# The context's keys, values and output matrix computed beside the q, k, v projection instead of inside the attention turns

## What is computed

```python
x = x + attention(layernorm(x), Wqkv, ...)        # q, k, v = clip(ln(x) @ Wqkv.T); 32 heads, causal, alibi
x = x + cross(layernorm(x), ctx, ctx, Wq, Wk, Wv, Wo, bo, g)
x = x + ffn(layernorm(x), ...)                    # 4-bit weights, hidden size 2752

def cross(q, k, v, ...):                          # per tile: arrays are 128 x 1024
    qh = softmax(Wq q over the 64 of a head) * SCALE
    kh = softmax(Wk k over the 1024 columns)      # 512 x 1024
    vh = Wv v
    context = kh vh^T per head                    # 8 blocks of 64 x 64
    out = Wo (context^T qh) + bo                  # then a norm over 128, times g
```

## Time and profile before

| | |
|---|---|
| median of 3 runs | 3303.19 us (3303.15 to 3303.97) |
| span of the profiled execution, first to last instruction | 3299.9 us |
| what lies around the span, against the median | 3.3 us |
| phase 1, first product to last | 24.07 to 561 us |
| phase 2, first turn to the last | 589 to about 1802 us |
| phase 3 | from about 1816 us |
| PE busy over the span | 3128.8 us (95%) |
| DVE, ACT, POOL busy | 1773.3, 1045.8, 507.1 us |

### The profile page before, as it was taken

How to read it: one execution, slowest core, us unless ns; L and a number is a source line. 1 busy time by engine, 2 the same in 40 slices (tenths; PEclk the granted TensorE clock), 3 DMA queues, 4 the chain that set the end, 5 groups by cost and what they waited for, 6 DMA issues and landing times. The chain is left out here.

```text
span 3299.9 us, 41826 instructions
## 1 busy us (share of the span) xinstructions
PE 3128.8 (95%) x15136; PEld 2393.9 (73%) x15136; DVE 1773.3 (54%) x2927; ACT 1045.8 (32%) x2356; POOL 507.1 (15%) x525
## 2 busy tenths in 40 slices
PE   7999997799999999999996799999999899999998
PEld 6888886566666666666663688888887788888887
DVE  5311112466666666666663655555555655555555
ACT  2100000566665566666651211111111211111111
POOL 2100000233333333333332100000000100000000
PEclk9999999899999999999996899999999999999999
DMA  4222223111111111111110432222122521231222
GB/s 144 93 73 75 73 70 116 41 39 38 43 46 51 38 38 39 50 38 51 38 33 31 129 82 55 76 65 75 54 82 76 153 64 54 81 81 54 62 74 78
DMA packets 83350, 218.73 MB, mean 66 GB/s; under 512 B 11984, under 2 KB 18256, under 8 KB 81232
## 3 DMA queue, kind: packets, MB, share of 16 engines
q1 hardware_dynamic: 83280, 217.78, 21.8%
HBM read 175.79 MB, written 41.94 MB: 66 GB/s over the span
## 5 line engine op out<-in xcount | busy, mean ns | idle before, releaser
L312 PE MATMUL ff_ps<-h_xT_hi,w_hi 128*128 128x512 f32 x1376 | 538.2, 391 | 13.2 <-DVE h_xT_lo L96 13.2
L312 PE MATMUL ff_ps<-h_xT_lo,w_hi 128*128 128x512 f32 x1376 | 537.1, 390 | 0.0
L312 PE MATMUL ff_ps<-h_xT_hi,w_lo 128*128 128x512 f32 x1376 | 537.0, 390 | 0.0
L1042 ACT ACTIVATE w_hi<-words 128x1024 fp32r<-128x1024 f32 x134 | 142.5, 1063 | 697.3 <-DVE words L1087 697.3
L1127 DVE TENSOR_TENSOR acc<-ff_po,acc 128x512 f32<-128x512 f32 x352 | 243.0, 692 | 210.6 <-PE ff_po L312 209.9
L312 PE MATMUL qkv_acc<-w_hi,xT_hi 128*128 128x512 f32 x768 | 300.9, 392 | 9.2 <-DVE w_lo L255 9.2
L312 PEld LDWEIGHTS ff_ps<-h_xT_hi,w_hi 128*128 128x128 f32 x1376 | 259.5, 189 | 68.3 <-issue 8.8
L312 PE MATMUL qkv_acc<-w_hi,xT_lo 128*128 128x512 f32 x768 | 299.4, 390 | 0.0
L312 PE MATMUL qkv_acc<-w_lo,xT_hi 128*128 128x512 f32 x768 | 299.3, 390 | 0.0
L312 PEld LDWEIGHTS ff_ps<-h_xT_hi,w_lo 128*128 128x128 f32 x1376 | 259.4, 189 | 54.1
L312 PEld LDWEIGHTS ff_ps<-h_xT_lo,w_hi 128*128 128x128 f32 x1376 | 259.6, 189 | 53.8
(11 more groups left out here) (156 smaller groups left out, 5305.9 us busy)
## 6 DMA issues: line engine op xcount, KB each, us to landing
words<-in_w SPq DMA_DIRECT2D x90, 512.0 KB, 3.5
qkv<-qkv_out SPq DMA_DIRECT2D x96, 256.0 KB, 2.0
words<-in_w SPq DMA_DIRECT2D x176, 128.0 KB, 4.0
sc<-in_s SPq DMA_DIRECT2D x88, 256.0 KB, 4.3
qk_in<-qkv SPq DMA_DIRECT2D x16, 1024.0 KB, 4.9
w_stage<-in_w_attn SPq DMA_DIRECT2D x56, 256.0 KB, 3.0
qkv_rows<-in_x SPq DMA_DIRECT2D x16, 512.0 KB, 3.8
ctx_in<-in_context SPq DMA_DIRECT2D x16, 512.0 KB, 3.7
```

The source lines that it names most:

```text
L312: last = nc.tensor.matmul(out, left, right, start=n == 0, stop=n == len(pairs) - 1)
L1042: nc.scalar.activation(dst, src, ACT.Copy).then_inc(s["split_hi"], 1)
```

## The change

Phase 1 becomes `projection_phase`. The 8 tiles of one half stay in SBUF at a time, so the 6 chunks of weights are loaded and split twice: 12 rounds of 8 steps. The buffer for weights is still two pieces, and now one piece is loaded and split in every step. Output gets two `res` buffers, the accumulators shrink from four banks to two. The first chunk is loaded into its own room (`kT`, unused then) with no wait between its pieces. In round 5 the second half of x is normalised and transposed.

In rounds 1 to 4 and 7 to 10, four steps belong to one tile's context (64 steps, quarter i = 0 to 3 of tile b): PE puts the key product ahead of the step's 24 matmuls, and the transposes of kE after the first 12. M is one product of 8 float32 matmuls of 128x512 in step i = 0 of the next tile. z goes to the new DRAM tensor zc and phase 2 loads it, one 256 KB tile per turn. From phase 2 the branch is removed, with its loads and waits; the next q and k are now loaded once their buffer has been transposed, since it no longer holds ctxT and M.

The diff, cut to its core:

```diff
+    TILES = NB // 2
+    ROUNDS = 2 * QKV_CHUNKS
+    CTX_ROUNDS = (1, 2, 3, 4, 7, 8, 9, 10)
...
+            def load(ci, r):
+                sp.wait_ge(s["w_lo_done"], ci * KT + r - 1)
+                chunk = ci % QKV_CHUNKS if ci < ROUNDS else QKV_CHUNKS
+                sp.dma_start(stage[:, r % 2, :], w_attn[chunk, :, r, :]).then_inc(w_in[r % 2], 16)
...
+            for ci in range(ROUNDS):
+                for t in range(TILES):
+                    at = ci * TILES + t
+                    b, i = step(ci, t)
+                    load(ci + 1, t)
...
+                    if i == 3 and b + 2 < NB:
+                        load_context(b + 2)
+                    if i == 0 and b >= 2:
+                        store_z(b - 2)
+                    sp.wait_ge(s["clipped"], at + 1)
+                    sp.dma_start(qkv[ci // QKV_CHUNKS * TILES + t, :, ci % QKV_CHUNKS * N:(ci % QKV_CHUNKS + 1) * N],
+                                 res[:, at % 2, :]).then_inc(stored[at % 2], 16)
...
         def _(act):
+            for ci in range(ROUNDS):
+                if ci:
+                    act.wait_ge(s["mm_done"], ci * TILES)
+                for t in range(TILES):
+                    b, i = step(ci, t)
+                    if i == 2 and b < NB:
+                        context(b)
...
+                    high(ci + 1, t, w_hi[1 - ci % 2])
+                    if b is not None and b < NB:
+                        exponential(b, i)
+                        turned(b, i)
...
         def _(dve):
+                        if b < NB:
+                            key_maxima(b, i)
+                        if i == 3 and b:
+                            blocks_out(b - 1)
+                        if i == 2 and b:
+                            sums(b - 1)
...
+                    low(ci + 1, t, w_hi[1 - ci % 2], w_lo[1 - ci % 2])
+                    if i == 0 and b:
+                        product_out(b - 1)
+                    dve.wait_ge(s["mm_done"], at + 1)
...
+            def keys(b, i):
...
+                for e in range(2):
+                    last = nc.tensor.matmul(room_k[:, e * N:(e + 1) * N], wk_sb[:, i * P:(i + 1) * P],
+                                            ctx_in[:, b % 2, e * N:(e + 1) * N], start=True, stop=True)
...
+            def turn_keys(b, i):
+                n = b * XT + i
+                pe.wait_ge(s["k_exped"], n + 1)
...
+            def key_context(b):
...
+                for k in range(KT):
+                    last = nc.tensor.matmul(room_u[:, 0:N], ctxT[:, k, :], kT[:, k, :], start=k == 0, stop=k == KT - 1)
...
+                    if b is not None and b < NB:
+                        keys(b, i)
+                    if at >= 2:
+                        pe.wait_ge(s["clipped"], at - 1)
+                    part(ci, t, range(KT // 2))
+                    if i == 0 and b:
+                        key_context(b - 1)
+                    if b is not None and b < NB:
+                        turn_keys(b, i)
+                    part(ci, t, range(KT // 2, KT)).then_inc(s["mm_done"], 1)
+                    if i == 1 and b < NB:
+                        turn_context(b)
+                    if i == 2 and b:
+                        values(b - 1)
+                    if i == 3 and b:
+                        outputs(b - 1)
...
     def turn_sync(sp, b, own, cross, ahead):
...
         if ahead:
-            sp.wait_ge(s["k_done"], (b + 1) * XT)
-            sp.dma_start(ctx_in[:, :], ctx_kv[b + 1, :, :]).then_inc(s["ctx_loaded"], 16)
-            sp.wait_ge(s["b_done"], b + 1)
+            sp.wait_ge(s["a_done"], 2 * b + 2)
             sp.dma_start(qk_in[:, :, :], qkv[b + 1, :, 0:2 * D].rearrange("p (a d) -> p a d", a=2)).then_inc(
                 s["qk_loaded"], 16)
             sp.wait_ge(s["o_done"], b + 1)
+            sp.dma_start(v_in[:, :], qkv[b + 1, :, 2 * D:3 * D]).then_inc(s["v_loaded"], 16)
+        if cross:
+            if own:
+                sp.wait_ge(s["y_done"], c + 1)
+        if own and cross:
+            sp.dma_start(z[:, :, :], zc[b, :, :].rearrange("p (a d) -> p a d", a=XT)).then_inc(s["z_loaded"], 16)
...
     def turn_tensor(pe, b, own, cross, ahead):
-            if own and (i := k_tile(t)) is not None:
...
-            if own and (i := kt_tile(t)) is not None:
...
-            if own and (i := m_tile(t)) is not None:
...
-            if own and t == STEPS - 2:
...
-            if own and t == STEPS - 1:
...
         if cross:
             pe.wait_ge(s["d_out"], (c + 1) * KT)
+            pe.wait_ge(s["z_loaded"], (c + 1) * 16)
```

More of the change, by code:

```diff
@@ L174, in qkv_phase, with step, before, first_stage @@
     w_in = [sem(f"w_in{i}") for i in range(2)]
[L175 to L187, removed]
+    w_first = [sem(f"w_first{r}") for r in range(KT)]
+    ctx_loaded = [sem(f"ctx_loaded{p}") for p in range(2)]
+    stored = [sem(f"qkv_stored{p}") for p in range(2)]
+    names = ("w_hi_done w_lo_done mm_done clipped setup_in filled k_done k_maxed k_exped kt_done kt_out c_done c_out "
+             "m_done m_out b_done b_out k_recced z_done z_ready z_stored").split()
+    s = {n: sem("p_" + n) for n in names}
+    def step(ci, t):
+        if ci in CTX_ROUNDS:
+            at = CTX_ROUNDS.index(ci) * TILES + t
+            return at // XT, at % XT
+        if ci == ROUNDS - 1 and t < XT:
+            return NB, t
+        return None, None
+    def before(ci, t):
+        return (ci, t - 1) if t else (ci - 1, TILES - 1)
+    def first_stage(r):
+        return kT[:, r, :]
     with nc.Block() as block:
@@ L228, in _, with high @@
         def _(act):
[L229 to L234, removed]
+            def high(ci, r, dst):
+                if ci:
+                    act.wait_ge(w_in[r % 2], ((ci - 1) * (KT // 2) + r // 2 + 1) * 16)
+                    src = stage[:, r % 2, :]
+                else:
+                    act.wait_ge(w_first[r], 16)
+                    src = first_stage(r)
+                nc.scalar.activation(dst[:, r, :], src, ACT.Copy).then_inc(s["w_hi_done"], 1)
@@ L235, in _, with context @@
+            def context(b):
+                act.wait_ge(s["c_done"], b + 1)
+                nc.scalar.activation(flat(ctxT[:, :, :]), room_u[:, :], ACT.Copy).then_inc(s["c_out"], 1)
+            for r in range(KT // 2):
                 high(0, r, w_hi[0])
             ln.high(act, 0, 0, turn[0])
-            for r in range(PIECES // 2, PIECES):
+            for r in range(KT // 2, KT):
                 high(0, r, w_hi[0])
[L240 to L244, removed]
-                        ln.high(act, t + 1, t + 1, turn[(t + 1) % 2])
-                    if t % 2 == 0:
-                        high(c + 1, t // 2, w_hi[1 - parity])
@@ new lines, in _ @@
+            for ci in range(ROUNDS):
+                for t in range(TILES):
+                    at = ci * TILES + t
+                    b, i = step(ci, t)
+                    if ci:
+                        was, quarter = step(*before(ci, t))
+                        if quarter == 3 and was:
+                            z_out(was - 1)
+                    if b is not None:
+                        if b < NB:
[4 more added lines that the diff above has]
+                            sums(b - 1)
+                    if ci == 0 and t + 2 < TILES:
@@ L275, in chunk @@
                         statistics(t + 2)
-                    if first and t + 1 < NB:
+                    if ci == 0 and t + 1 < TILES:
                         ln.low(dve, t + 1, t + 1, turn[(t + 1) % 2])
[L278 to L283, removed]
@@ L287, in _ @@
+                    nc.vector.tensor_scalar(res[:, at % 2, :], acc[:, at % 2, :], CLIP, -CLIP, ALU.min,
+                                            ALU.max).then_inc(s["clipped"], 1)
+                    if ci == 5:
+                        ln.low(dve, TILES + t, t, turn[t % 2])
         @block.tensor
         def _(pe):
-            pe.sem_inc(clipped, BANKS)
-            ln.transpose(pe, 0, 0, turn[0])
-            def chunk(c, parity, first):
-                for t in range(NB):
-                    if first and t + 1 < NB:
-                        ln.transpose(pe, t + 1, (t + 1) % 2, turn[(t + 1) % 2])
[L296 to L304, removed]
```

405 lines of the change are left out of this document (222 added, 183 removed).

## The result

The changed kernel takes 3624.36 us (3623.73 to 3625.11), the kernel before 3303.17 us in the same comparison: a ratio of 1.0971, 95% interval 1.0958 to 1.0985. The forecast was 3585 us, its range 3490 to 3665. The profiled execution has a span of 3622.0 us, 322 more than before.

What follows compares the result with a forecast made beforehand. PE was taken to bound both phases, with a DVE and ACT loop bounding the turns after the change. 3299.9 + 374 (phase 1) - 77 (15 turns) - 15 (turn 0) = 3582 us span, 3585 with 3.3 around it; range 3490 to 3665.

Steps and rivals of the forecast that it cites:

- Both stages were bound by PE: Phase 1 and the turns: PE busy 536.63 of 536.93 us and 628.72 of 655.72 us, so PE bounds both.
- 333 us for the branch in phase 1: Phase 1: the context's PE work, 20.8 us times 16 contexts, is paid in full; bounds +320 and +350.
- Waits for kE, 47 us, and 2 us for the loads elsewhere: Phase 1: PE waits 3.0 us per context for the keys' exponential; the load loop adds 2 us in steps without context.
- First product 8 us earlier: Start of phase 1: the first chunk no longer waits for pairs of buffers, -8 us, bounds 0 and -12.
- Steps of 4.21 us by the loop: Steps of a turn: a closed loop over DVE and ACT takes 4.21 us a step, against PE's 3.04.
- A turn of 65.2 us and 2.5 for the clock: Phase 2: 65.2 us plus 2.5 for PE's lower clock gives 67.7 a turn, from 72.9; -77 us over 15.
- The run-out to y: End of a turn's steps: cross tiles 6 and 7 run out before y starts, 9.6 us.
- Turn 0: -15: First turn of phase 2, without q work: 68 us before, shorter by 15, bounds -5 and -20.
- Rival 1: Turns: PE stays the bound, a turn is 47.6 us and the time 3282, faster; 4 in 100.
- Rival 2: Phase 1: the wait for weights is hidden, time 3538 us; 15 in 100.
- Rival 3: Steps: PE's clock falls, turns of 71 to 73 us, 3635 to 3665; or loads land late, 3633; 20 in 100.
- The signs: Expected observations: phase 1 ending near 935 us, turns 65 to 68 us apart, PE idle a quarter of the turn.

Runs made afterwards that it cites:

- E10: The kernel before, with DVE's sum and reciprocal of q moved behind the bias and maxima of the scores: 3328.2 us, ratio 1.0071.
- E9: The changed kernel with SP's load of the next piece of weights issued one step earlier, ahead of the store: 3549.7 us, ratio 1.0739.
- E8: E3 with SP's load of the next piece of weights issued one step earlier, ahead of the store: 3295.0 us, ratio 0.9974.
- E1: The changed kernel with the keys' exponential ahead of the copy of weights in ACT's queue: 3558.1 us, ratio 1.0767.
- E3: The changed kernel's phase 1 in halves without the branch, followed by the kernel before's attention phase with the branch: 3310.8 us, ratio 1.0018.
- E4: The changed kernel with DVE's sum and reciprocal of q moved behind the bias and maxima in the turns: 3577.2 us, ratio 1.0828.
- E6: E5 with four more unread matmuls (0.9 us) in each of steps 3 to 7 of each full turn: 3598.6 us, ratio 1.0896.
- E5: The changed kernel with 16 more matmuls, result not read, in each full turn where PE waits: 3599.2 us, ratio 1.0886.

## Why the prediction was right, step by step

The sign, the size and the mechanism were as forecast. Of the span 40 us were missed, some 23 of them in the turns and 17 in phase 1 and up to the first turn. Part of the closeness is luck: the branch was priced 7 us too high, which hides some of 24 us that were missing from the waits.

- **Both stages were bound by PE.** Held. In the turns of the kernel before, E10 finds no gain in the order that relieves DVE and ACT, and what PE loses by it shows in the time.
- **333 us for the branch in phase 1.** Measured 326 (E9 less E8). The distances between starts of the earlier trace rows were good to 2%.
- **Waits for kE, 47 us, and 2 us for the loads elsewhere.** The mechanism held, place by place: 49 waits, of 1.6, 0.8 and 0.8 us in quarters 1, 2 and 3, with the copy of weights ahead of the exponential. Mis-sized: 73 us together (the changed kernel less E9) for 49. E1 takes 65 of the 73: the records show 52.7 us of idle time, the distances between starts 60.5. The other 8 are what the early load still gains behind E1, for 2 in the sum. A loop of 5.5 us against a step of 5.44 gives 6 us over 96 steps; E3 lost 16, since the loop came to 5.66 on average.
- **First product 8 us earlier.** Measured 9.0.
- **Steps of 4.21 us by the loop.** Measured 4.24. E4 and E6 show from both sides that it is the bound: a change of DVE's order moves it, 0.9 us of PE does not.
- **A turn of 65.2 us and 2.5 for the clock.** Measured 69.1, or 69.3 over turns 1 to 14 (table at E5). The steps were right. The clock took 3.0 us at two places. One was foreseen, the matmuls behind the wait ahead of y (2.1). The other was not: at the start of a turn the scores of group 2 run at the low level, and DVE waits for them (0.9), although the prediction had the scores never waited for. The run-out to y was 0.7 us longer than worked out; that stays open. By its own terms the sum to group 2 is 4.5 + 3.3 + 3.3 = 11.1 us, not 11.3. A turn too short by 1.4 us is 21 us of the miss; most of the rest comes from taking the 72.9 us of nine turns for all 15, which take 72.6.
- **Turn 0: -15.** Measured -15.2.
- **Rival 1, PE stays the bound:** refuted by E6. **Rival 2, the wait is hidden (3538):** it was not, but E9 is that kernel, 3549.7. **Rival 3, the clock falls in the steps (turns of 71 to 73):** partly. The granted clock is 0.92 in the turns, but steps 3 to 7 have slack for it, so that only the start of a turn and y paid.
- **The signs.** Phase 1 ended at 950.8 us for "near 935", PE's idle share of the turns was 19% for a quarter, and turns were 69.1 us apart, just above the 65 to 68 given.

The Trainium skill, page "TensorE: Matmul & The Clock Gate", section "A second HAM failure mode: psum-queue depth-cycling", tells of an engine that idles shortly between groups of matmuls and swings between its clock levels, and of throughput lost so. The trace agrees: the mean clock is 0.99 before, 0.92 after and 0.98 with fillers, and within one turn it goes from 0.50 to 1.00 and back. How much throughput was lost is read from E5 alone: 3.0 us of a 69 us turn.

## What to carry to other kernels

Moving work off a full engine in one stage onto a full engine in another is paid in full at the new place; at the old place it gives back only the distance to the next bound, so look for the closed loop of the other engines (from one instruction to its next self) before the work is moved. An instruction that needs only on-chip data should not queue behind one that waits for a load (66 us here), and a load should be issued ahead of the store it does not depend on, which alone took 75 us off here and made the first remedy needless. An order of instructions that helps one bound can hurt the other (-47 and +24 us for the same edit).

## What the runs showed of the hardware

- Added matmuls made the kernel faster: 16 float32r matmuls a turn in PE's waits raised the granted clock from 0.92 to 0.98 and took 25 us from the time, though the waits that they don't fill stayed as long.
- In phase 1, 49 waits with 52.7 us of idle time between the records cost 60.5 us by the distances between starts, and removing them took 65 us off the phase (E1).
- Matmuls at the low clock cost time only where something waited for them: in the changed kernel the scores of group 2 and y, 3.0 us a turn. Steps 3 to 7 take 21.3 us in it and 21.2 in E5.
- 12 MB more of weights (E8) did not slow the products at all: 443 matmuls in 100 us at a DMA share of 0.36, as many as the kernel before has at 0.22 (124 to 224 us).
